# Row tiles for pairs of attention scores, block transposes on VectorE, and a new order of the step

## The reference

```python
Q = layernorm(x) @ Wq.T + bq        # 100 x 256 for each of 16 batches
K = ctx @ Wk.T + bk                 # 361 x 256
V = ctx @ Wv.T + bv
dot = einsum("bhsd,bhtd->bhst", Q, K) / sqrt(16)
o = einsum("bhst,bhtd->bhsd", softmax(dot), V).reshape(B, 100, 256)   # heads are NOT moved back: rows are of (h, s) order
x = x + tanh(g_xattn) * (o @ Wh.T + bh)
x = x + tanh(g_ffn) * experts(layernorm(x))    # top 2 of 8 low-rank experts over a 256 -> 1024 -> 256 gated MLP
```

## Time and profile before

| what | value |
|---|---|
| time, median of 3 runs | 507.66 us (506.61 to 508.35) |
| the profiled execution's own time | 509.6 us |
| its span, first to last instruction | 507.7 us |
| mean granted TensorE clock | 0.993 of full |
| one step of the attention loop, mid-kernel | 13.2 us |
| busy: TensorE, VectorE, ScalarE, GpSimd | 96%, 70%, 53%, 56% of the span |

### The profile page before, as it was taken

How to read it: one execution, slowest core, us unless ns; L and a number is a source line. 1 busy time by engine, 2 the same in 40 slices (tenths; PEclk the granted TensorE clock), 3 DMA queues, 4 the chain that set the end, 5 groups by cost and what they waited for, 6 DMA issues and landing times.

```text
span 507.7 us, 11754 instructions
## 1 busy us (share of the span) xinstructions
PE 487.7 (96%) x4350; PEld 456.2 (90%) x4350; DVE 357.9 (70%) x768; ACT 266.6 (53%) x584; POOL 282.4 (56%) x339
## 2 busy tenths in 40 slices
PE   7888999999999999999899999999999999999996
PEld 6657999999999999997789999899999999999994
DVE  6866777877878877888577869856486456854444
ACT  4456766666676777667666533443335333233331
POOL 5645666666666666561676536644386444854440
PEclk9989999999999999999989999999999999999999
DMA  7793786677777777553601000010000100001001
GB/s 199 180 289 93 216 214 153 157 182 190 189 179 180 180 176 169 120 111 57 204 10 17 1 0 1 1 34 0 1 0 2 34 1 1 0 2 34 0 1 32
DMA packets 51144, 45.83 MB, mean 90 GB/s; under 512 B 33935, under 2 KB 40115, under 8 KB 51088
## 3 DMA queue, kind: packets, MB, share of 16 engines
q1 hardware_dynamic: 41310, 23.18, 19.6%
q0 software_dynamic: 7504, 18.69, 14.1%
q10 hardware_dynamic: 2274, 3.21, 2.0%
HBM read 20.59 MB, written 6.66 MB: 54 GB/s over the span
## 4 chain that ended last, share of the span: by engine, by line
PE 84%; DVE 6%; DMA 5%; issue 2%; ACT 2%; POOL 1%; ACTq 0%; DVEq 0%
PE bank L1368 14%; PE bank L1223 7%; PE bank L1246 7%; PE bank L1372 7%; PE bank L1385 6%; PE bank L1420 6%; PE bank L1205 6%; PE bank L1259 6%; PE bank L1193 5%; PE bank L1400 4%; DMA QS<-crow 3%; PE bank L1292 3%; PE bank L1403 2%; PE bank L1180 2%; PE bank L1335 2%
## 5 line engine op out<-in xcount | busy, mean ns | idle before, releaser
L970 DVE TENSOR_REDUCE nmax<-bank 100x1 f32<-100x361 f32 x256 | 130.0, 529 | 38.4 <-PE bank L1223 33.4
L419 POOL TENSOR_TENSOR awl<-hb,awh 128x400 fp32r<-128x400 f32 x63 | 70.2, 1114 | 109.4 <-ACT awh L627 109.4
L529 ACT ACTIVATE pt<-bank 120x400 f32<-120x400 f32 (+1 forms) x192 | 90.3, 503 | 25.8 <-PE bank L1246 12.2
L627 ACT ACTIVATE awh<-hb 128x400 fp32r<-128x400 f32 x64 | 34.5, 539 | 119.0 <-DVE hb L906 118.7
L1223 PE MATMUL bank<-KS,QS 96*100 96x362 f32 x256 | 86.9, 358 | 5.2 <-DVE nmax L970 4.8
L899 DVE TENSOR_TENSOR hb<-sil,bank 128x400 f32<-128x400 f32 x64 | 36.5, 570 | 73.7 <-PE bank L1385 37.9
L1246 PE MATMUL bank<-QS,KS 97*120 97x200 f32 (+1 forms) x384 | 66.4, 271 | 1.6 <-ACT pt L529 1.0
L1246 PEld LDWEIGHTS bank<-QS,KS 97*120 97x120 f32 (+1 forms) x384 | 60.2, 184 | 2.8 <-DMA QS<-crow 1.7
L328 POOL TENSOR_TENSOR cth<-craw,cth 128x724 fp32r<-128x724 f32 x16 | 27.7, 1729 | 63.0 <-ACT cth L475 54.8
L1223 PEld LDWEIGHTS bank<-KS,QS 96*100 96x100 f32 x256 | 41.6, 167 | 12.8 <-DVE nmax L970 7.3
L333 POOL DMA_DIRECT2D QS<-q_dram x90 | 46.0, 519 | 0.4 <-issue 0.3
(11 more groups left out here) (221 smaller groups left out, 1116.3 us busy)
## 6 DMA issues: line engine op xcount, KB each, us to landing
KS<-kn SPq DMA_DIRECT2D x128, 90.5 KB, 3.3
KS<-kn POOLq DMA_DIRECT2D x64, 90.5 KB, 3.4
craw<-ctxT POOLq DMA_DIRECT2D x14, 361.0 KB, 4.9
QS<-q_dram POOLq DMA_DIRECT2D x92, 50.0 KB, 3.6
q_dram<-qn ACTq DMA_DIRECT2D x4, 400.0 KB, 4.1
o_dram<-on SPq DMA_DIRECT2D x16, 100.0 KB
xr<-o_dram SPq DMA_DIRECT2D x16, 100.0 KB
y<-xs SPq DMA_DIRECT2D x8, 200.0 KB
```

The costliest lines, as they stand in the source:

```text
L419: nc.gpsimd.tensor_tensor(awl[:, g % 2, slot], hb[:, slot], awh[:, g % 2, slot].bitcast(F32), ALU.subtract).then_inc(m["p_awl"], 1)
L529: nc.scalar.activation(pt[0:TW[t], u, :], pT[u % 3][0:TW[t], 0:CS], ACT.Exp, scale=float(DH) ** -0.5).then_inc(m["act_e"], 1)
L970: nc.vector.tensor_reduce(nmax[:, h // 8, pos % 8:pos % 8 + 1], pS[h % 2][0:S, 0:T], AX.X, ALU.max, negate=True).then_inc(m["dve_s"], 1)
```

## The change

Four things at once.

**Scores in pairs.** The four rows 4r to 4r + 3 of KS and QS now hold the terms of one element (high, high, low, and one unused), so that the two heads of a pair lie in rows 0 to 63 and 64 to 127. `s_pair` issues two matmuls, one on rows 0 to 62, one on rows 64 to 126, into two of three banks. The maxima's row is 127, KS is filled with ones at first (by VectorE and GpSimd instead of by two DMAs), and the copies go to every fourth partition. The third score bank is taken from the units, which now have two.

**Block transposes.** VectorE's `nc.vector.transpose` turns the sums in 32x32 blocks straight from pO (128x416) to oT; `o_turn` and ScalarE's copy go. Reciprocal and product work on 128 partitions. Each of the 13 blocks per group of four heads holds 32 positions of the reference's order, so xr is read in two halves (104 rows), and `turned_o` is two strided copies.

**Values in four parts**, after units 2, 5, 8 and 11 as far as the order of exponentials allows, and the head order of Q, K and V changed to fit.

**A new order** of `body` on PE, VectorE and ScalarE; steps 14 and 15 keep the old one but for the parts that go.

```diff
-        pS, pT, pO, pP = ps[0:2], ps[2:5], ps[5], ps[6:8]
+        pS, pT, pO, pP = ps[0:2], ps[2:4], ps[5], ps[6:8]
+        s_bank = lambda b, h: ps[h % 2] if b == 0 else ps[(0, 1, 4)[((b - 1) * H + h) % 3]]
...
             def k_stack(b, g):
-                for row in (0, 32):
-                    sp.dma_start(KS[b % 3][row:row + 32, g, :, :].rearrange("p j t -> p (j t)").bitcast(F32),
+                for term in range(2):
+                    sp.dma_start(KS[b % 3][term:128:4, g, :, :].rearrange("p j t -> p (j t)").bitcast(F32),
...
-                    sp.dma_start(o_dram[i - 1].rearrange("(h s) d -> s h d", h=H), on[:]).then_inc(m["xo"], 16)
+                    sp.dma_start(o_dram[i - 1].rearrange("c p d -> p c d"), on[:]).then_inc(m["xo"], 16)
...
-                    sp.dma_start(xr[:], o_dram[i - 1].rearrange("(r c) d -> r (c d)", c=H)).then_inc(m["xi"], 16)
+                    for half in range(2):
+                        sp.dma_start(xr[half * 4 * OC:(half + 1) * 4 * OC],
+                                     o_dram[i - 1].rearrange("c (g h p) d -> h g c (p d)", g=4, h=2)[half]).then_inc(m["xi"], 16)
...
             for n in range(3):
                 nc.gpsimd.memset(QS[n][:].bitcast(F32), 0.0).then_inc(m["zero"], 1)
+            for n in range(1, 3):
+                nc.gpsimd.memset(KS[n][:].bitcast(F32), 1.0).then_inc(ones_in, 1)
...
+            def blocks_turned(i):
+                dve.wait_ge(m["pe_pv"], i * UN)
+                wait(dve, "dve_on", i - 1)
+                nc.vector.transpose(oT[:].rearrange("p c d -> p (c d)"), pO[:, 0:OC * 32]).then_inc(m["dve_o"], 1)
...
+            def s_one(b, h):
+                g, odd, j = h // 4, h % 2, h % 4 // 2
+                row = slice(64 * odd, 64 * odd + 63)
+                mm(s_bank(b, h)[0:S, 0:TP], QS[b % 3][row, g, odd, j, :], KS[b % 3][row, g, j, :],
+                   start=True, stop=True).then_inc(m["pe_s"], 1)
...
+            def s_pair(b, p):
+                s_ready(b, 2 * p)
+                pe.wait_ge(m["dve_s"], b * H + 2 * p - (0 if b == 1 and p == 0 else 1))
+                s_one(b, 2 * p)
+                s_one(b, 2 * p + 1)
...
-                wait(pe, "act_e", n - 2)
+                wait(pe, "act_e", n - 1)
```

More of the change, by code:

```diff
@@ L639, in body, with late_step @@
                 b = i + 2
[L640 to L643, removed]
+                row_copy(i, 1)
+                row_send(i, 1)
+                expo(i, 0)
+                k_high(b, 0)
+                expo(i, 1)
+                expo(i, 2)
+                k_high(b, 1)
+                expo(i, 3)
+                expo(i, 4)
+                if has_c(i):
+                    ctx_high_of(i + 3)
+                expo(i, 5)
+                wait(act, "pe_pv", i * UN)
+                v_out(b, 0)
+                expo(i, 6)
+                row_copy(i + 1, 0)
+                expo(i, 7)
+                row_send(i + 1, 0)
+                expo(i, 8)
+                v_out(b, 1)
+                expo(i, 9)
+                expo(i, 10)
+                expo(i, 11)
+                v_out(b, 2)
+                if i == 0:
+                    q_store(2)
+                    act.wait_ge(m["sm_in"], 4 * 16)
+                    nc.scalar.activation(tgx[:], gx[:], ACT.Tanh).then_inc(m["tg_ok"], 1)
+                    nc.scalar.activation(tgf[:], gf[:], ACT.Tanh).then_inc(m["tgf_ok"], 1)
+                if i == 1:
+                    q_store(3)
+                if i == B - 3:
+                    for k in range(4):
+                        normed_x(0, k)
+            def late_step(i):
+                b = i + 2
                 row_out(i, 1)
@@ L1027, in body, with late_step @@
                 head(i + 1, 0)
+                if has_o(i):
+                    blocks_turned(i)
+                head(i + 1, 1)
+                head(i + 1, 2)
+                if has_o(i):
+                    shares(i)
+                k_low(b, 0)
+                head(i + 1, 3)
+                head(i + 1, 4)
+                k_low(b, 1)
+                head(i + 1, 5)
+                head(i + 1, 6)
+                head(i + 1, 7)
+                head(i + 1, 8)
+                head(i + 1, 9)
+                head(i + 1, 10)
+                head(i + 1, 11)
+                head(i + 1, 12)
+                if has_y(i):
+                    turned_o(i)
+                head(i + 1, 13)
+                if has_o(i):
+                    quotient(i)
+                head(i + 1, 14)
+                head(i + 1, 15)
+                if i >= 3:
+                    variance(i - 3)
+                if i == 1:
+                    dve.wait_ge(m["pe_y"], 1)
+                    dve.wait_ge(m["tg_ok"], 1)
+                    nc.vector.tensor_tensor(bhs[:], pP[1][0:S, 0:D], bhs[:], ALU.add).then_inc(m["bh_ok"], 1)
+                    dve.wait_ge(m["bh_ok"], 1)
+                    nc.vector.tensor_scalar(tbh[:], bhs[:], tgx[0:S, :], None, ALU.mult).then_inc(m["tbh_ok"], 1)
+                elif has_y(i):
+                    first_sum(i)
+                if i in (11, 12):
+                    for k in range(7 * (i - 11), 7 * (i - 11) + 6):
+                        root(0, k)
+                if i == 11:
+                    root(0, 6)
+            def late_step(i):
+                b = i + 2
+                if has_o(i):
+                    blocks_turned(i)
+                head(i + 1, 0)
                 head(i + 1, 1)
@@ L1087, in last_step @@
                 variance(13)
-            for i in range(0, B - 1):
+            for i in range(0, B - 2):
                 body(i)
+            late_step(B - 2)
             last_step(B - 1)
@@ L1201, in v_part @@
             def v_part(b, t, p0, p1):
[L1202 removed]
+                bank = (pS[0], pS[1], ps[4])[t] if b == 0 else pP[1] if b == 1 and t == 1 else pP[0]
                 for p in range(p0, p1):
```

277 lines of the change are left out of this document (143 added, 134 removed).

## The result

The changed kernel takes 532.71 us (median of 4, 530.21 to 534.95) beside 507.68 us; the ratio is 1.0494, 95% interval 1.0443 to 1.0545. It is 25 us slower where 12 us faster was forecast, and beyond the range. The first rival, the drain, had named 523 us.

The account below looks back on a forecast made before the run. TensorE was taken to bound the kernel, its step falling from 13.22 to 12.35 us; gains of 9.6, 1.5, 0.5, 0.4 and 0.35 less 0.3 for startup gave 12.05 us, so 495.6 us, range 489 to 521.

Parts of the forecast that it names:

- The first rival, the drain: Score pairs: each switch to half-height tiles and back costs 0.33 us a pair; 523 us, chance 0.24.
- What bounds the kernel: Attention loop: TensorE, busy all of the 13.22 us step, sets its length; VectorE has 10.66 us of work, ScalarE 8.97.
- The price of going to half-height tiles: Score pairs on TensorE: 0.05 us a pair taken, between ends of 0 and 0.33; 8 pairs add 0.40 us a step.
- the upper end: Score pairs: 0.33 us a pair, from 0.15 around the values, 0.10 weight load behind and 0.08 scaled going in.
- The rival's sum: Loop step if pairs drain TensorE: 13.22 - 1.78 + 2.44 + 0.40 = 14.3 us; chance 0.24.
- Its sign: Drain at the score pairs: weight-load queue idle before and behind every pair, slots of 0.4 us and more; chance 0.24.
- Two heads in one slot: Score matmuls: two heads run side by side, so 8 slots of 0.167 us go, -1.34 us a step.
- Values in four parts: Values on TensorE: one excursion becomes three, each extra one 0.20 us, +0.40 us a step.
- Sums turned by VectorE: Loop step: TensorE loses 0.44 us; VectorE's transpose takes 0.59 us, its work rising from 10.66 to 11.4 us.
- Startup: Before the loop: GpSimd's two added memsets may share with a VectorE cast, +0.3 us, between 0 and 0.4.
- The sum: Whole kernel: steps, expert part and startup together gain 12.05 us, giving a median of 495.6 us.
- Transfers, banks, DMA: Loop: transfers cost 0, hidden behind TensorE; stalls from two exponential banks add 0.10 us a step.

Follow-up runs that it names:

- the second and third transpose runs: Kernel before with only VectorE's block transposes, the transpose moved behind the tenth head (second, 512.96 us) or behind the eighth (third, 510.25 us).

## Why the prediction was wrong

- **What bounds the kernel: right.** The changed kernel's step is TensorE's bill, to 0.1 us: 13.22 us before, less 0.44 for the turns, plus 0.24 for the values (2.44 against 2.20), plus 0.05 for the pairs' slots (8 x 0.34 against 16 x 0.167) and 1.50 behind them is 14.57; measured 14.60. The forecast had -1.34 + 0.40 for the pairs, the runs show +1.55.
- **The price of going to half-height tiles: the step that failed.** I took 0.05 us a pair, "nearest to the alternation of 96 and 128 rows that costs nothing". The runs show 0.34 to 0.36 us an excursion (entry 0.17, way back 0.17 to 0.19): the upper end, 0.33, that I had worked out from the values (that it is met so closely is partly luck, as 0.08 of it was scaled). 96, 97, 127 and 128 rows follow each other without a gap; 63 rows do not. The choice between the ends went by likeness of shape, when the row that had the same kind of cut was the one around the values. The rule of the Trainium skill that I weighed against this choice (TensorEngine Tiling (Array Packing), Tiling Modes) says that a change of tiling mode drains TensorE; the trace agrees for the cut by rows too (0.34 to 0.36 us an excursion, weight loads idle on both sides). The rival's sum, 14.3 us a step, was 0.3 short. Its sign, slots of 0.4 us and more, did not show: the slot is 0.34 us, and the other half of the price lies in what follows.
- **Two heads in one slot: right**, worth 0.15 us a pair of the 0.167 expected. It is less than half of an excursion's price, so a pair of 362 columns loses.
- **Values in four parts: mis-sized.** 0.40 us taken; it is 0.24 us in the changed kernel, where the pair behind pays for an excursion anyway, and 0.24 + 0.34 = 0.58 us with whole-row scores.
- **Sums turned by VectorE: right in its price** (0.61 us against 0.59, the two copies 0.43 us together against 0.50), and TensorE did lose the 0.44 us. But VectorE's place mattered: alone, the step fell by 0.20 us at best. The average of 11.4 us of work did not show that within the first 2 us of the step VectorE is the one that is late.
- **Startup: failed.** I saw that VectorE might share with the memset and put 0.3 us on it. The loop starts 8.6 us later. The addition that waited 3.41 us, with the low clock behind TensorE's idle time, is 3.0 to 4.7 us of it; whole rows give 1.1 to 1.7 us (52.0 against 54.0 less the 0.96 us by which TensorE's first turns came earlier; 47.6 against 49.3); the rest goes with the clock from 25 to 47 us (0.84 against 0.92) and is not taken apart further. I had looked at one VectorE cast beside the memsets, not at the five small additions and scalings (6.7 to 8.3 us before) on which everything behind them hangs.
- **The sum.** Expected -12.05, measured +25.4 us in the span: +8.6 before the loop; in the loop 13 intervals between blocks of values grew from 13.45 to 14.68 us on average (+16.0), the rest of it and the experts add 0.8.
- **Transfers, banks, DMA: right** for the changed kernel; at 14.6 us a step nothing waits for them. At 13.0 us a step some steps wait for them (the second and third transpose runs).

## What to carry to other kernels

Before packing matmuls into tiles, look in the trace for any excursion to another tile shape and price a round trip there (here 0.34 us), including the time in which the weight loads stand idle. Here two matmuls of 362 columns save 0.15 us a trip. So three pairs behind each other should be the least that pays, an estimate from these two numbers: no run here puts pairs next to each other, and in this kernel VectorE's 0.44 us a head would hold them back. A long memset on GpSimd is not free beside VectorE: place it where VectorE runs no small addition on a chain, or cut it into pieces. And when the start of a kernel moves, read the granted clock of several executions before putting the difference down to the edit.

## What the runs showed of the hardware

- Matmuls of 96, 97, 127 and 128 rows follow each other with no gap; 63 rows at row 0 or 64 cost 0.17 us in and up to 0.19 us out, even for a single matmul, and even directly behind the quarter-column values (a pair there takes 0.34 us as elsewhere).
- A whole-row matmul with 100 columns of weights behind the values takes 0.17 us more (0.50 against 0.33 for two).
- In TensorE's records such switches count as busy; the weight loads' idle time (0.23 and 0.17 us) and the spacing of the chain's pieces show them.
- A VectorE addition of 100x4 took 3.41 us behind two 2.5 us memsets on GpSimd, 0.21 us among sixteen of mostly 0.40 us, 0.17 us with none, and in one execution 0.95 us, to the end of the first memset; statistics beside them ran at their usual length.
- Eight matmuls of the query projection (L1278) took 4.85 us in the changed kernel's startup from 14.36 us on, at a granted clock that was half of full until about 18.2 us, and 2.92 us at the full clock before. TensorE had been idle for 5.15 us ahead of it.
